# Fewer gathers queued: six block gathers ahead of TensorE for 32, and row gathers two at a time

## What is computed

```python
xf = x.reshape(-1, C)                                   # 4096 tokens, C = 256
shared = silu(xf @ w1) * (xf @ w3) @ w2                 # shared expert, hidden size 512
s = sigmoid(concatenate([xf, tf], -1) @ router_W)
_, topk_idx = top_k(s + router_bias, 2)                 # two of eight experts for each token
combine = zeros((N, 8)).at[arange(N)[:, None], topk_idx].add(gates)
h = gelu(einsum('nc,ech->enh', xf, W1e))                # expert hidden size 256
y = einsum('enh,ehc->enc', h, W2e)
return (shared + einsum('ne,enc->nc', combine, y)) / 3
```

## Time and profile before

| | |
|---|---|
| median of 3 runs | 3083.74 us (3081.33 to 3088.0) |
| the profiled execution | 3087.38 us, of which the span of the trace is 3085.5 us |
| mean granted clock of TensorE | 0.966 of 2.4 GHz |
| TensorE busy | 2856.8 us, 93% of the span |
| VectorE, ScalarE, GpSimd busy | 1924.5, 1206.9, 475.3 us |
| TensorE's share of the chain that ended last | 86% |
| TensorE busy in the first 425 us | 345.7 us |
| TensorE busy in the other 2660.5 us | 2511.1 us |

### The profile page before, as it was taken

One profiled execution on the slowest core, in us unless ns is written; L12 is line 12 of the kernel. 1 busy time (PEld: TensorE's weight loads), 2 busy tenths in 40 slices (PEclk: granted clock), 3 DMA queues, 4 the chain that ended last, 5 costly groups with the idle time before them and its releaser, 6 DMA issues.

```text
span 3085.5 us, 72545 instructions
## 1 busy us (share of the span) xinstructions
PE 2856.8 (93%) x28542; PEld 2200.1 (71%) x28542; DVE 1924.5 (62%) x6596; ACT 1206.9 (39%) x2713; POOL 475.3 (15%) x608
## 2 busy tenths in 40 slices
PE   8597897999999999999999999978999858999998
PEld 4496356777777777777777777645666638999998
DVE  4263357777777777777777777555667654444444
ACT  1132232333434333343433433234555514555554
POOL 0633400000000000000000000012433212333333
PEclk9798898999999999999999999999999968999999
DMA  3434300101001010100101011111222132222222
GB/s 137 132 110 171 98 23 1 36 22 32 22 33 35 23 32 22 33 29 27 34 22 32 22 33 36 34 37 39 67 74 60 47 107 45 35 39 38 37 39 32
DMA packets 93314, 148.90 MB, mean 48 GB/s; under 512 B 19936, under 2 KB 76128, under 8 KB 89760
## 3 DMA queue, kind: packets, MB, share of 16 engines
q1 hardware_dynamic: 72720, 107.83, 10.6%
q0 software_dynamic: 20112, 36.40, 5.7%
q10 hardware_dynamic: 144, 0.03, 0.0%
HBM read 95.93 MB, written 48.27 MB: 47 GB/s over the span
## 4 chain that ended last, share of the span: by engine, by line
PE 86%; DVE 6%; issue 2%; ACT 2%; another core or an unknown queue 1%; DMA 1%; SPq 0%; DVEq 0%; POOLq 0%; ACTq 0%
PE ps L994 15%; PE ps L813 14%; PE ps L2044 8%; PE ps L1059 8%; PE ps L2059 8%; PE ps L1028 4%; PE ps L975 4%; PE ps L416 2%; PE ps L427 2%; PE ps L274 2%; PE ps L263 2%; PE ps L262 2%; PE ps L843 2%; PE ps L844 2%
## 5 line engine op out<-in xcount | busy, mean ns | idle before, releaser
L813 PEld LDWEIGHTS ps<-arena 128*128 128x128 f32 x4096 | 538.0, 193 | 30.2 <-ACT arena L821 3.3
L994 PE MATMUL ps<-arena 128*128 128x256 f32 x2048 | 551.2, 393 | 1.2 <-DVE arena L1004 1.0
L813 PE MATMUL ps<-arena 128*128 128x128 f32 x4096 | 541.1, 276 | 2.9 <-ACT arena L821 2.9
L994 PEld LDWEIGHTS ps<-arena 128*128 128x128 f32 x2048 | 355.5, 190 | 163.1 <-issue 133.3
L821 ACT ACTIVATE arena<-ps 128x256 f32<-128x256 f32 x512 | 196.4, 384 | 546.6 <-PE ps L813 546.2
L1059 PE MATMUL ps<-arena 128*16 128x256 f32 x4096 | 271.3, 382 | 10.3 <-DVE arena L1089 9.8
L2044 PE MATMUL ps<-arena 128*128 128x128 f32 x2272 | 267.2, 276 | 0.7 <-DVE arena L2116 0.7
L2044 PEld LDWEIGHTS ps<-arena 128*128 128x128 f32 x2272 | 261.2, 193 | 1.2 <-DVE arena L2116 1.1
L2059 PE MATMUL ps<-arena 128*128 128x256 f32 x1136 | 256.8, 379 | 0.0
L1777 POOL MEMSET arena<- 128x3072 f32 x1 | 2.7, 2659 | 1633.3 <-PE ps L994 1633.3
L1080 DVE SCALAR_TENSOR_TENSOR arena<-arena 128x128 f32<-128x128 f32 x256 | 73.9, 288 | 280.3 <-ACT arena L1071 280.3
(11 more groups left out here) (286 smaller groups left out, 4712.4 us busy)
## 6 DMA issues: line engine op xcount, KB each, us to landing
xw_scratch<-arena SPq DMA_DIRECT2D x32, 512.0 KB, 2.7
arena<-xw_scratch SPq DMA_DIRECT2D x256, 64.0 KB, 2.7
arena<-in_W SPq DMA_DIRECT2D x16, 1024.0 KB, 5.2
ys_scratch<-arena SPq DMA_DIRECT2D x71, 128.0 KB, 1.7
xn_scratch<-arena SPq DMA_DIRECT2D x32, 129.0 KB, 2.6
arena<-in_xT SPq DMA_DIRECT2D x8, 512.0 KB, 8.3
arena<-in_kinT SPq DMA_DIRECT2D x1, 4096.0 KB
arena<-in_xtb SPq DMA_DIRECT2D x32, 128.0 KB, 2.2
```

The lines of the kernel that those rows point to most:

```text
L813: m = e.matmul(bank(b)[:, 128 * i:128 * i + 128], kin[:, k, 2 * jp + i, :], xcT[:, k, 128 * blk:128 * blk + 128], start=(k == 0), stop=(k ...
L994: m = e.matmul(bank(7)[:, 0:256], G[blk % 2][:, j, :], kout[:, j, :], start=(j == 0), stop=(j == 31))
```

## The change

The change sets NXA to 6, so POOL's block gather n waits for the transposes of block n - 6. The row gathers are numbered j = 0 to 63. From j = 2, gather j waits until gather j - 2 has landed. Gather j raises semaphore `xs{j % 8}`, so the eight of one call now lie on eight semaphores, and the engines that weigh them wait on all eight. The wait for `c_tr` stays where it was.

```diff
-        NXA = 32
+        NXA = 6
...
         def rows_gpsimd(e, n):
             if n >= 4:
                 e.wait_ge(s["c_tr"], 2 * n - 6)
-            for m in range(4 * n, 4 * n + 4):
-                for k in range(2):
-                    row_gather_gpsimd(e, ya[m][:, k], ysd, slot[:, k, m:m + 1], s[f"xs{n}"])
-
-        def rows_count(n):
-            return 16 * uses(NBK, n, 8) + 128
+            for j in range(8 * n, 8 * n + 8):
+                if j >= 2:
+                    e.wait_ge(s[f"xs{(j - 2) % 8}"], row_count(j - 2))
+                row_gather_gpsimd(e, ya[j // 2][:, j % 2], ysd, slot[:, j % 2, j // 2:j // 2 + 1], s[f"xs{j % 8}"])
+
+        def row_count(j):
+            return 16 * uses(NBK, j % 8, 8) + 16 * (j // 8 + 1)
...
         def weigh_scalar(e, n):
             e.wait_ge(s["rg"], 12)
-            e.wait_ge(s[f"xs{n}"], rows_count(n))
+            for j in range(8 * n, 8 * n + 8):
+                e.wait_ge(s[f"xs{j % 8}"], row_count(j))
...
         def weigh_vector(e, n):
             e.wait_ge(s["ym"], n + 1)
-            e.wait_ge(s[f"xs{n}"], rows_count(n))
+            for j in range(8 * n, 8 * n + 8):
+                e.wait_ge(s[f"xs{j % 8}"], row_count(j))
...
+            for i in range(8):
+                e.wait_ge(s[f"xs{i}"], 16 * uses(NBK, i, 8))
             for n in range(8):
-                e.wait_ge(s[f"xs{n}"], 16 * uses(NBK, n, 8))
                 rows_gpsimd(e, n)
...
-            return rows_count(n % NX) + 16 * (n // NX + 1)
+            return row_count(56 + n % NX) + 16 * (n // NX + 1)
```

## The result

| | before | after |
|---|---|---|
| median | 3083.64 us (3081.33 to 3088.0, 4 runs) | 3029.18 us (3027.99 to 3031.61, 4 runs) |
| span of the trace | 3085.5 us | 3027.3 us |
| mean granted clock | 0.966 | 0.977 |
| TensorE busy | 2856.8 us | 2851.8 us |

The ratio is 0.982, with a 95% interval of 0.981 to 0.984: 54 us less, where 66 were forecast. The time lies inside the range, 11 us above the 3018 us forecast. How much of it belongs to the place where it was measured is the subject of the experiments.

A forecast was written before the change was run, and what follows sets the result against it. TensorE, busy 93%, bounds the kernel, idling on counts delayed by gather trains. Savings of 34 + 32 = 66 us take the profiled 3087.4 us to 3021, or 3018 us on the median; range 3005 to 3058 us.

The forecast's parts named there:

- The cause of the stalls: First 425 us: long back-to-back gather trains on POOL make TensorE's counts arrive late; TensorE idles 79 us.
- rival 3: Gathers and late counts share a common neighbour (big loads, program code being fetched); neither goes, 3084 us; chance 4%.
- Six ahead: Block gathers: the TensorE stall from 94.3 to 133.2 us goes, saving 34 us.
- The allowance of 2 us for the first ten gathers: Block gathers: 2 us off 35.8 us, since the first ten still come back to back and some counts may be late.
- The stall before tile 3's output: TensorE's 26.7 us idle between tile 3's products and its output at 315.25 us, expected to go.
- The cap: Two row gathers in flight, tiles 3 to 7: costs 8 us of the 40.1 us available, leaving 32 us.
- Gather 16: Row gathers beside the big loads: five or so pairs land in about 26 us, gather 16 near 309 us, old clock.
- The other 48 gathers: Row gathers after gather 16: 1.45 us each, the last landing near 379 us, 5 us late.
- The sum of 66 us: Whole kernel: 34 us from the block gathers plus 32 us from the row gathers.
- Rival 1: Row gathers still stall the counts, so only the first part is gained: 3050 us; chance 26%.
- Rival 2: The first stall, near 95 us, stays in part, one or two steps costing 12 to 24 us: about 3035 us; chance 8%.
- Rival 4: Row gather pairs are slow, 3.65 us per gather, stage ends 58 us later: 3141 us; chance 4%.

The follow-up runs named there:

- stalling places: Places where the kernel before took 3083.64 us (first comparison) or 3085.02 us (chip 5).
- quiet places: Four chips (0, 12, 6 and 4) where the kernel before took 3008.13, 3008.46, 3008.02 and 3009.7 us.
- chip 12: Unchanged kernel before again, 3008.16 us; changed kernel again, 3027.79 us, ratio 1.0065; three row gathers in flight instead of two, 3012.96 us.
- chip 5: Changed kernel with four row gathers in flight instead of two: 3044.46 us, ratio 0.987 to the kernel before at 3085.02 us.

## Why the prediction was right, and where its numbers were off

**The cause of the stalls.** The prediction had counts of TensorE that arrive late while POOL gathers back to back. In the stalling places this held: neither kernel with six ahead had a stall at 94 us there, and with four in flight there was a second stall that two in flight did not have. It isn't the whole cause. The quiet places have longer trains and no stall, so a part of rival 3 was right: something beside the gathers decides too. The prediction weighed it as a neighbour inside the program, at 4%, and had no thought of a property of the place. One profiled kernel on one chip could not show it. That the forecast was confirmed is in part luck: the change was measured where the kernel before takes 3084 us. On chip 12 its time, 3027.79 us, lies in the same range, but it is 19 us slower there than the kernel before and not faster.

The rule cited at rival 3, that a DMA isn't slowed by compute and vice versa (the Trainium skill, SBUF — State Buffer, SBUF: two separate sides), agrees with the four quiet chips. On chip 5 TensorE stood 27.30 us while gathers ran, but no instruction took longer: ScalarE's late copies at 288.62 and 308.92 us last 0.60 us like the others. What came late was the end of a wait, of which the rule says nothing, so rival 3 did not follow from it.

**Six ahead: 34 us, measured 36.8.** The last L427 ended at 267.7 us before (265.85 + 1.89) and at 230.9 now (229.05 + 1.89). The allowance of 2 us for the first ten gathers is seen at 92.79 and 94.51 us, but the whole is 1.0 us more than the window had shown to be available. The windows behind the stall show what that sum had left out, first before, then after:

```profile
133.20:140.00 6.80, 6.78 (x31) 6.05 (x32) 3.71 (x9) 2.12 (x6) 2.85 (x3) 0.66 0.27 86
```

```profile
133.20:140.00 6.80, 6.80 (x51) 6.31 (x50) 4.31 (x11) 2.69 (x7) 3.54 (x4) 1.00 0.44 125
```

After the stall TensorE still ran at clock 0.66 and made 20 matmuls fewer, 2.8 us at 7.13 per us. The prediction counted such matmuls in the tiles, but not here. In a quiet place the same edit is worth 0.

**The stall before tile 3's output.** 26.7 us were expected to go, and went: the output follows L536's last product without a gap.

**The cap: 8 us, measured 18.** This is the step that was off, and the signs that were to show it missed too: tiles 4 to 7 were to take 22.5 to 26 us, and two took 31.45 and 27.72 us. The windows lose 8.9 + 2.0 + 5.2 + 1.9 = 18.0 us against 22.52 each. Two terms were too small. Gather 16 was to land 20.4 us after tile 3's last product, at 272 us on the new clock. ScalarE starts on it at 277.21 us, 5 us later: three pairs beside the loads took 24.6 us, from 235.37 to 259.98 us, where the prediction had put five or so into 26 us at 5.0 us each. The other 48 gathers were to take 1.45 us each. They took (353.63 - 277.21) / 48 = 1.59 us, 6.8 us more in all. The term rested on a landing of 2.6 us read from a stretch of silence, where the row allowed 2.1 to 3.1; the upper half was right. The estimate of 2.3 us for 128 KB from the Trainium skill's figures (DMA: Bandwidth & Descriptors, Anatomy of one DMA) was further off: 2.7 us is the median on chip 12. The two terms come to some 12 us where 10 are missing, so the other terms of that sum were about 2 us too large together. The sum of 66 us loses 10 by this and gains 2.8 from the blocks: 59, which is what the stage's end shows (425.84 to 366.85 us). The profiled executions differ by 58.3 us, the medians by 54.5: the profiled one of before lay 3.6 us over its median, as the prediction had noted.

**The rivals.** Rival 1 did not happen, but its mechanism is the one that the run on chip 5 shows: the unbroken train does harm, in quiet and with four in flight. Of the prediction's two arguments against it, the one that gathers pile up behind big loads has fallen, since on chip 5 they stall without such loads. The other, that pairs break the train, stands. By these runs 1.5 to 1.6 us per gather, each waiting for a landing, is on the good side and 1.25 on the bad one; rival 1 had put the pairs nearer to the bad. Rival 2 is seen only as 2.57 us at 92.79 us. Rival 4 is what happens in the quiet places, at a smaller price: not 3.65 us per gather but 1.6, and 19 us in all. There the kernel before has already the 3008 us that the prediction named as the most that could be gained.

**A version that beats both** wasn't found for every place. In the quiet ones four in flight, at 3010 us, is level with the kernel before; in the stalling ones two, at 3029 us, is the best measured and 15 us ahead of four, each measured in another stalling place. Three in flight goes at 1.25 us per gather in quiet and wasn't run in a stalling place. Nor was a pace set by TensorE, between 1.41 us and 1.6.

## What to carry to other kernels

Space out a queue of gathers by the consumer's count, as the six blocks do: it costs nothing where nothing stalls (three comparisons within 0.1%) and saved 36.8 us where it did. A cap on transfers in flight is another thing: a gather takes at least the landing time over the number in flight, so work that out with the landing under load before choosing the cap. In the quiet places two in flight cost 19 us and three 4.5. And time the kernel before in more than one place before a stall in its profile is taken for the kernel's own.

## What the chip showed that was not expected

- The same program takes 3008 to 3010 us on four chips and 3085 on another, with each set of runs within 9 us. In the traces the difference lies in counts that arrive late while POOL issues gathers.
- In a stalling place the late counts come in long steps, 14 us in before and 20.30 us (288.62 to 308.92) with four in flight, and end with the train.
- About ten gathers at 1.25 us do little harm there, more do: ScalarE idles 2.57 us at the end of a train of nine in the changed kernel, while the first count to be late by 8 us or more was raised some twelve gathers into its train both in the kernel before (at 96.8 us) and with four in flight (near 278 us).
- A 128 KB row gather lands in 2.7 us in the median of the changed kernel on chip 12; a pair beside 9 MB of loads takes up to 9.8 us.
- Why some places stall stays open. The landing records missing from their traces are the one other sign, and it is there without a stall too.
